# Local attention: the gelu of a sequence moves from the end of its gate step to the middle of the next step

## The reference

```
def attn_layer(x, Wqkv, qs, ksc, Wo):
    qkv = x @ Wqkv
    q, k, v = jnp.split(qkv, 3, -1)
    ...
    q = l2norm(q) * qs
    k = l2norm(k) * ksc
    ...
    out = local_attention(q, k, v)
    ...
    return out @ Wo

def ffn_layer(x, g, bln, W1, b1, W2, b2):
    ...
    hg = xn @ W1 + b1
    a, gate = jnp.split(hg, 2, -1)
    return a * jax.nn.gelu(gate, approximate=False) @ W2 + b2
for i in range(DEPTH):
    x = attn_layer(shift_tokens(x), Wqkv[i], q_scale[i], k_scale[i], Wo[i]) + x
    x = ffn_layer(shift_tokens(x), ln_g[i], ln_b[i], W1[i], b1[i], W2[i], b2[i]) + x
```

## Time and profile before

| | |
|---|---|
| median of 3 runs | 5318.9 us (5310.04 to 5323.08) |
| the profiled execution | 5318.81 us, span 5317.0 us, mean granted TensorE clock 0.943 |
| TensorE busy | 4797.5 us, 90% of the span |
| VectorE busy | 3247.7 us, 61% |
| GpSimd busy | 2772.0 us, 52% |
| ScalarE busy | 2369.9 us, 45% |
| gelu L576 | 48 times, 1485 ns each, and 46 table loads of 1283 ns before it |
| exp L572 | 192 times, 1056 ns each, and 46 table loads of 1283 ns before it |
| local attention stage, steady part | about 860 to 2420 us and 3600 to 5200 us |

### The profile page before, as it was taken

The page is one execution under the profiler, slowest core; times in us unless marked ns, Lnnn a source line. Parts: engine busy times, 40 slices in busy tenths (PEclk is TensorE's granted clock), DMA queues, the critical chain, the costliest instruction groups (busy, mean ns, idle before and its releaser), DMA issues. The chain is left out here.

```text
span 5317.0 us, 123357 instructions
## 1 busy us (share of the span) xinstructions
PE 4797.5 (90%) x51848; PEld 3296.1 (62%) x51848; DVE 3247.7 (61%) x4325; ACT 2369.9 (45%) x2803; POOL 2772.0 (52%) x3572
## 2 busy tenths in 40 slices
PE   7799789999999999997688888789999999999996
PEld 3332356666666666664577777466666666666664
DVE  1365166666666666673566665366666666766663
ACT  2344145555555555553211111055555555555553
POOL 0000087777777777773111110187777777777772
PEclk9799889999999999998799998699999999999998
DMA  0000000000000000000000000100000000000000
GB/s 12 5 1 1 31 21 18 2 14 10 15 10 14 10 6 2 2 2 1 8 0 0 0 0 0 40 10 18 2 14 10 15 10 14 10 6 2 2 2 9
DMA packets 15066, 46.11 MB, mean 9 GB/s; under 512 B 4176, under 2 KB 6992, under 8 KB 12752
## 3 DMA queue, kind: packets, MB, share of 16 engines
q1 hardware_dynamic: 14544, 38.67, 2.1%
HBM read 37.61 MB, written 1.05 MB: 7 GB/s over the span
## 5 line engine op out<-in xcount | busy, mean ns | idle before, releaser
L718 POOL TENSOR_TENSOR w_qk<-w_turned 128x1024 f32<-128x1024 f32 x384 | 905.2, 2357 | 267.3 <-DVE w_turned L601 217.9
L596 DVE TENSOR_TENSOR w_turned<-w_ps_qk,w_rot_l 128x1024 f32<-128x1024 f32 x384 | 469.9, 1224 | 839.3 <-ACT w_squares L498 819.3
L305 PE MATMUL w_ps_y<-w_px,w_w_vo 128*128 128x128 f32 x6144 | 789.7, 284 | 116.3 <-ACT w_px L502 116.0
L305 PEld LDWEIGHTS w_ps_y<-w_px,w_w_vo 128*128 128x128 f32 x6144 | 754.0, 200 | 151.6 <-ACT w_px L502 130.3
L255 PE MATMUL w_ps_qk<-w_w_qk,ZT 128*128 128x512 f32 x1536 | 751.2, 612 | 37.3 <-DVE w_turned L601 17.2
L747 POOL TENSOR_TENSOR w_qk<-w_qk,w_inv_norm 128x1024 f32<-128x1024 f32 x384 | 723.3, 1906 | 0.0
L498 ACT ACTIVATE w_squares<-w_ps_qk 128x1024 f32<-128x1024 f32 x384 | 391.5, 1020 | 548.2 <-PE w_ps_qk L255 547.8
L601 DVE TENSOR_TENSOR w_turned<-w_ps_qk,w_rot_l 128x1024 f32<-128x1024 f32 x384 | 466.5, 1215 | 0.0
L605 DVE TENSOR_REDUCE w_sumsq<-w_squares 128x16 f32<-128x1024 f32 x384 | 455.3, 1186 | 0.0
L255 PEld LDWEIGHTS w_ps_qk<-w_w_qk,ZT 128*128 128x128 f32 x1536 | 266.5, 194 | 266.4 <-issue 242.1
L261 PE MATMUL w_ps_t<-ident,w_qk 128*128 128x128 f32 x3072 | 418.1, 280 | 5.4 <-ACT w_qT L531 5.4
(11 more groups left out here) (258 smaller groups left out, 9058.8 us busy)
## 6 DMA issues: line engine op xcount, KB each, us to landing
w_w_qk<-in_w_qk SPq DMA_DIRECT2D x12, 1024.0 KB, 4.9
w_w_vT<-in_w_vT SPq DMA_DIRECT2D x12, 512.0 KB, 3.5
w_w_o<-in_w_o SPq DMA_DIRECT2D x12, 512.0 KB, 5.2
w_w<-in_w SPq DMA_DIRECT2D x12, 384.0 KB, 3.0
w_w<-in_w SPq DMA_DIRECT2D x12, 192.0 KB, 3.1
XT<-in_x SPq DMA_DIRECT2D x1, 1024.0 KB, 4.8
w_rot<-in_rot SPq DMA_DIRECT2D x2, 512.0 KB, 6.1
out<-XT SPq DMA_DIRECT2D x1, 1024.0 KB, 4.8
```

The source lines that it names most:

```text
L305: last = nc.tensor.matmul(ps_y[:, D.t * P:(D.t + 1) * P].rearrange("p (a v q) -> p a v q", a=2, q=WIN), w_vo[:, D.parity, h, p, :], px[:, ...
L596: nc.vector.tensor_tensor(turned[:, which, 0, :].rearrange("p (h d) -> p h d", d=DH), flat(ps_qk[:]).rearrange("p (h d) -> p h d", d=DH), ...
L718: nc.gpsimd.tensor_tensor(qk[:, T.odd, which, :], turned[:, which, 0, :], turned[:, which, 1, :], ALU.add).then_inc(pool_add, 1)
```

## The change

The gelu's three lines leave the end of `s.gate`'s step on ScalarE. They come back in the next step, where the same sequence is `s.up`, behind the copy L538 of the transposed keys and ahead of the second `square`. The wait for `act_gate` has the same value, since both names stand for the same sequence. No other engine's code changes.

```diff
                     nc.scalar.activation(kT[:, :, HALO + B.t * P:HALO + (B.t + 1) * P], turned_k,
                                          ACT.Copy).then_inc(act_tk, 1)
+                if s.up:
+                    f = s.up
+                    act.wait_ge(act_gate, f.m * FFB + FFB)
+                    nc.scalar.activation(flat(hid[:]), flat(hid[:]), ACT.Gelu).then_inc(act_gelu, 1)
                 if T:
                     square(T, 1, pe_k)
...
                 if B:
                     act.wait_ge(dve_sub, B.n + 1)
                     nc.scalar.activation(probs[:], probs[:], ACT.Exp).then_inc(act_exp, 1)
-                if s.gate:
-                    f = s.gate
-                    act.wait_ge(act_gate, f.m * FFB + FFB)
-                    nc.scalar.activation(flat(hid[:]), flat(hid[:]), ACT.Gelu).then_inc(act_gelu, 1)
```

## The result

| | before | changed |
|---|---|---|
| median | 5315.5 us (4 runs, 5310.04 to 5323.08) | 5149.05 us (4 runs, 5143.61 to 5153.77) |
| profiled execution, and its span | 5318.81 us, 5317.0 us | 5153.77 us, 5151.9 us |
| mean granted TensorE clock | 0.943 | 0.952 |

The ratio is 0.9686, with a 95% interval of 0.9669 to 0.9702. The kernel is 3.1% faster; 5158 us had been forecast, with a range of 5148 to 5203.

What follows compares the result with a forecast made beforehand. TensorE was taken as the bound, losing time to its wait for px and clock falls: 114.4 us waiting, 41.0 clock and 5.4 tails make 160.8, so 5318.8 - 160.8 = 5158.0 us, range 5148 to 5203.

Steps and rivals of the forecast that it cites:

- the two bounds: Start of L305: ScalarE's L502 allows 1437.52, TensorE's own order 1437.61; the later counts, so L305 moves by 2.52 us.
- The size of the wait: Up step (behind the gate step, s.up set): L305 and L261 close up, 2.6 us per step, 44 full steps.
- The clock: TensorE's clock falls behind the wait in 24 of 44 full up steps; removing them saves 1.71 us each, 41.0 us.
- the clock doesn't follow: Rival: the wait goes but another short wait keeps the clock falling in about as many steps; 5199 us, chance 0.10.
- What is added: Load and gelu between L538 and the second square (L498) add nothing; bounds 0 to 0.3 us per up step.
- GpSimd: POOL's idle before L718 shrinks to 0.23 us; L757 ends 1.81 us earlier, margin 0.5 before L288; does not bind.
- L288 waits for POOL: Sign of being wrong: TensorE's transposes L288 of the probabilities waiting for GpSimd, where a margin of 0.5 was forecast.
- The rule of the Trainium skill: Rival on ScalarE: each table switch drains another 1.38 us, 2.66 in all; dearer switch or missed margin 5211 us, chance 0.06.
- emptying pipelines: First of the last two up steps per run: L502 starts 2.68 us earlier, 5.4 us in the two runs.
- POOL binds: Rival: `probs` from GpSimd come 0.8 us later than worked out, gain 2.3 per step, 5172 us, chance 0.07.
- the edit doesn't do what it says: Rival: something else holds ScalarE's copy L502 at its old place; 5319 us, chance 0.02.
- Slower: Rival: the gelu comes late for L612, which TensorE's second up product needs; 1 us more gives 5363 us, chance 0.01.

Runs made afterwards that it cites:

- the copy in the old place: Kernel before with a plain ACT.Copy instead of the gelu, in the old place, so no table loads in this stage: 5200.0 us, ratio 0.9783.
- a wait of 1.68 us: Kernel with gelu and load between the copy L502 of px and the copy of the transposed queries: 5231.0 us, ratio 0.9828 to the kernel before.
- the copy in the new place: Changed kernel with a plain ACT.Copy instead of the gelu, so its table loads in this stage go too: 5145.3 us, ratio 0.9685 to the kernel before.
- the second trace of the changed kernel: Changed kernel run once more, unedited, beside the repeat with one more copy: 5149.1 us, ratio 0.9689 to the kernel before.
- 3.03 us before L430: Changed kernel with the gelu's four lines one instruction further on, behind the second square: 5330.8 us, ratio 1.0029 to the kernel before.
- the kernel with 1.9 us of waiting: Kernel before with the gelu over two of its three blocks, in the old place, third block left out: 5283.7 us, ratio 0.9939.

## Why the prediction was right

**Where the wait is.** Right. TensorE's wait for `px` was the one that ended last, and L305 moved by what the two bounds gave.

**The size of the wait.** The prediction took 2.6 us per full up step. From the copy of the queries in the gate step to that in the up step the median went from 20.15 to 17.56 us in both runs of the stage, which is 2.59.

**The clock.** 24 falls of 1.71 us were to go, and they went. That this was a cost of its own and not part of the wait is shown by the copy in the old place: 0.93 us of waiting is left there, and the stage's gain of 107 us is the 63 of the wait and the 41 of the clock and 3 more. The rival "the clock doesn't follow" is out, also for a wait of 1.68 us.

**What is added.** Right in its sum, nothing. The pair is hidden: the loads by the copy in the new place, the whole by its rows and by the gelu ahead of the keys' copy, all within 5 us. One step of it was wrong. I called the late square covered because L612 ends behind it, and counted only the gelu's margin of 0.55 us. The square ends at 1416.38 in the changed kernel and the rotation starts at 1416.68, so its margin is 0.30. Behind the rotation VectorE has no idle time: the second L612 ends at 1419.68, and TensorE's third up product starts 0.06 us later. Half a microsecond more in this place costs about 10 us in all, where my accounting said none. The edit itself stays inside both margins.

**GpSimd.** Right to a few hundredths in the step worked out: 0.23 us idle before L718, and a margin of 0.51 us before L288 where 0.5 had been worked out. "L288 waits for POOL" had been named as a sign of being wrong. It does so in 3 of the 44 full up steps of the trace (8 in the second trace of the changed kernel), for 0.15 to 0.25 us, under 2 us in all. The one step was taken for all of them; it changes nothing in the sum.

**What a switch costs.** ACT's rows show 0.02 us between the end of the keys' copy and the load, and 0.02 between load and gelu. The rule of the Trainium skill that the prediction kept as a rival ("ScalarE: Activation LUTs", "What ACT_TABLE_LOAD costs") would put 1.38 us more there; the trace doesn't agree in this place either. The prediction's own figure of 1.29 us was a little low for a switch that is waited for. In the kernel with the copy in the old place the exp starts at 1561.67 and the copy at 1562.61, 0.94 apart, where exp and gelu were 2.37 apart before; that and the wait that went from 2.35 to 0.93 both say 1.42 to 1.43 us. Without a load between them the second instruction starts 0.12 us before the first has ended.

**The sum.** From the first projection of a run to the last addition of its feed-forward, the two traces give 68.9 us less in the first run and 89.1 in the second, 158.0 together; forecast were 160.8. By parts:

| | forecast | traces |
|---|---|---|
| steps 2 to 97, waits and clock | 155.4 | 149.4 |
| emptying pipelines | 5.4 | 8.1 |
| filling pipelines | 0 | 0.6 |
| everything outside the stage | 0 | 7.0 |

The steps fell short by 6 us. In this pair of traces 5.3 us more of stalls would account for most of it. The wait of TensorE put down to "issue" before the scores grew, over the whole span, from the first row (before) to the second (changed):

```profile
PE w_ps_s L280 <- issue: 8.2, 14, 1.2
```

```profile
PE w_ps_s L280 <- issue: 13.5, 21, 1.1
```

But the second trace of the changed kernel has 10.6 us in 19 such stalls, and its two runs of the stage take 6.4 us less than the first trace's. Differences of this size lie within the spread of executions, and no run shows that the edit causes them. The emptying pipelines gave 2.7 us more. 1.7 of these are the clock, which is low for 3.4 us less there; the prediction had left that term out of its sum. The last line of the table is not the edit's: no code outside the stage changed, and the profiled execution of before was simply 7.5 us later at the first projection. Over the 13 traces the time outside the stage lies between 1565 and 1580 us, and that of before is the longest. Single executions of the kernel before lie between 5302 and 5327 us in these sets. So the trace pair agrees with the forecast within 3 us inside the stage (with the second trace of the changed kernel it is 164.5 against 160.8), which is closer than the spread allows one to claim. The 166 us between the medians hold a few microseconds that no step of the prediction explains; that the time landed inside the range by 1 us is partly luck.

**Rivals.** "POOL binds" is out as a price, and "the edit doesn't do what it says" altogether, by the rows above. "Slower" was right as a mechanism and right to be given 0.01 for this place: one instruction further on it takes the whole gain back (5331 us).

## What to carry to other kernels

An instruction that nobody needs for half a step should stand in an idle time of its engine that is about as long as it is, and ahead of its reader's own wait. Both are read from one timeline: here 2.48 us of idle time for a pair of 2.77 us, 0.2 us over, with 0.3 and 0.55 us of margin behind it, and two such places gave the same time while their neighbours on either side lost half or all of it. Count the margin of everything that is pushed back to the next wait of the busiest engine, not just to the next instruction that looks free.

A short recurring wait of TensorE can cost more than its length: here 2.35 us cost 2.6 and, in 24 of 44 up steps, 1.7 of clock besides. In the kernel that kept 0.93 us of the wait at the same place the clock's part was given back in full before the wait was gone.

## What the runs showed of the hardware

The number of clock falls was graded and not all or nothing: before L305 none of 44 at 0.93 us of waiting, 18 at 1.9, and 24 at 2.35 and again at 2.38. There the price was the same each time, about 1.71 us; of the 32 falls at 3.03 us before L430 four cost twice that.

The stalls before the scores come near the end of a run of 128 equal matmuls, in the changed kernel as before:

```profile
1563.27 1.40 PE L280 MATMUL w_ps_s<-w_kT,w_qT 64*32 64x64 f32 x119
1565.57 0.32 PE L280 MATMUL w_ps_s<-w_kT,w_qT 64*32 64x64 f32 x9 [0.91 <-issue]
```

In this stretch TensorE executes 128 matmuls in 1.48 us when nothing holds it. In all 13 traces each such stall (0.15 to 1.2 us) comes before the 108th to the 122nd of them, and never earlier. What TensorE waits for there no run tested. An execution has 12 to 25 of them, 7.7 to 15.4 us in all. The changed kernel's two traces have 21 and 19, before has 14. But the kernel with 1.9 us of waiting has 19, and the changed kernel with one more copy 14 and 17, so that less waiting elsewhere brings more stalls is not shown.
